# First cross-attention of a decoder: another job order, another bank table, and the maximum in two pairs of heads

## What is computed

```python
y_dca, y_main = y[:, -16:, :], y[:, :-16, :]
q = ln((x @ Wq + bq) by head)            # 16 heads of 32
k, v = ln(y_main @ Wk + bk), y_main @ Wv + bv
k_dca, v_dca = ln(...), ...              # the last 16 rows of the context, weights of their own
ctx     = softmax(q k.T * scale) v          # over 240 keys
ctx_dca = softmax(q k_dca.T * scale) v_dca  # over 16 keys
x = layernorm(x + (ctx + ctx_dca) @ Wo + bo)
```

## Time and profile before

| | us |
|---|---|
| median of 3 runs | 2538.05 |
| the profiled execution | 2538.91 |
| its span, first to last instruction | 2537.0 |
| main loop of the first cross-attention | 505 to 990 of the span |

### The profile page before, as it was taken

One profiled execution on the slowest core, in us unless ns is written; L12 is line 12 of the kernel. 1 busy time (PEld: TensorE's weight loads), 2 busy tenths in 40 slices (PEclk: granted clock), 3 DMA queues, 4 the chain that ended last, 5 costly groups with the idle time before them and its releaser, 6 DMA issues. The chain is left out here.

```text
span 2537.0 us, 40781 instructions
## 1 busy us (share of the span) xinstructions
PE 2159.8 (85%) x15664; PEld 1831.0 (72%) x15664; DVE 1568.4 (62%) x3131; ACT 1215.2 (48%) x3223; POOL 762.9 (30%) x820
## 2 busy tenths in 40 slices
PE   5999998388888887499997879999999999966876
PEld 5898897266777766377776778888988988853443
DVE  3555664555656554788875645556666666656777
ACT  3555553366666653444333334445555554423466
POOL 2233332666666652044441111111111112220011
PEclk8999999689999987599998989999999999988999
DMA  3000000200000000711101031224324312101000
GB/s 133 1 2 1 2 1 1 75 5 5 5 5 6 5 1 4 256 65 34 34 18 46 1 133 59 93 84 145 113 84 146 112 68 76 51 1 67 6 29 34
DMA packets 42777, 127.17 MB, mean 50 GB/s; under 512 B 3917, under 2 KB 11086, under 8 KB 37593
## 3 DMA queue, kind: packets, MB, share of 16 engines
q1 hardware_dynamic: 42584, 124.56, 14.0%
HBM read 103.57 MB, written 20.97 MB: 49 GB/s over the span
## 5 line engine op out<-in xcount | busy, mean ns | idle before, releaser
L2003 POOL TENSOR_TENSOR x_probs<-x_probs,x_total 128x512 f32<-128x512 f32 x128 | 133.2, 1041 | 595.5 <-DVE x_total L1973 595.3
L1928 ACT ACTIVATE x_probs<-banks,x_nmax 128x256 f32<-128x256 f32 x256 | 119.0, 469 | 213.9 <-DVE x_nmax L1962 213.9
L133 ACT ACTIVATE x_probsT_hi<-banks 128x512 fp32r<-128x512 f32 x256 | 143.7, 607 | 106.8 <-PE banks L1862 101.2
L519 PE MATMUL banks<-x_probsT_hi,x_V_hi 128*128 128x256 f32 x512 | 160.6, 314 | 38.6 <-DVE x_probsT_lo L139 38.0
L139 DVE TENSOR_TENSOR x_probsT_lo<-banks,x_probsT_hi 128x512 fp32r<-128x512 f32 x256 | 165.1, 675 | 45.8 <-ACT x_probsT_hi L133 45.6
L519 PE MATMUL banks<-x_turned,x_wq_hi 128*128 128x256 f32 x1024 | 186.0, 283 | 8.2 <-DVE x_turned L139 8.2
L925 ACT ACTIVATE x_probs<-banks,x_nmax 128x240 f32<-128x240 f32 x256 | 114.4, 460 | 139.8 <-DVE x_nmax L955 139.8
L817 POOL TENSOR_TENSOR x_probs<-x_probs,x_total 128x960 f32<-128x960 f32 (+1 forms) x128 | 130.4, 1040 | 161.3 <-DVE x_total L967 161.3
L448 ACT ACTIVATE a_probs<-banks,a_nmax 128x128 f32<-128x128 f32 (+1 forms) x256 | 104.1, 419 | 126.9 <-DVE a_nmax L464 126.9
L519 PEld LDWEIGHTS banks<-x_turned,x_wq_hi 128*128 128x128 f32 x1024 | 156.8, 189 | 9.4 <-DVE x_turned L139 9.4
L504 POOL TENSOR_TENSOR a_probs<-a_probs,a_total 128x512 f32<-128x512 f32 x64 | 93.9, 1467 | 229.5 <-DVE a_total L474 229.5
(11 more groups left out here) (455 smaller groups left out, 7245.6 us busy)
## 6 DMA issues: line engine op xcount, KB each, us to landing
x_turned<-x_parked SPq DMA_DIRECT2D x24, 1536.0 KB, 6.8
x_parked<-x_turned SPq DMA_DIRECT2D x8, 1536.0 KB, 5.8
x_raw_q<-in_L_xattn_Wq_dram SPq DMA_DIRECT2D x5, 1024.0 KB, 5.2
x_raw_o<-in_L_xattn_Wo_dram SPq DMA_DIRECT2D x5, 1024.0 KB, 8.2
x_all<-in_x_dram SPq DMA_DIRECT2D x2, 2048.0 KB, 18.7
x_ys<-in_ctx_dram SPq DMA_DIRECT2D x16, 256.0 KB, 2.9
f_raw<-in_L_ffn_W_g_dram SPq DMA_DIRECT2D x4, 1024.0 KB, 7.0
f_raw<-in_L_ffn_W_u_dram SPq DMA_DIRECT2D x4, 1024.0 KB, 5.4
```

The lines of the kernel that those rows point to most:

```text
L133: return eng.activation(out, in_, ACT.Copy, scale=scale)
L519: ins = eng.matmul(out, lhs, rhs, start=start and n == 0, stop=stop and n == len(steps) - 1)
L1928: ins = eng.activation(probs[t][r][:, j, :], g.S[:, 2 * t + r, j * S:(j + 1) * S], ACT.Exp, bias=nmax[:, t, r, j:j + 1], accum_out=total[: ...
L2003: eng.tensor_tensor(probs[t][r][:, :, :], probs[t][r][:, :, :], total[:, t, r, :].unsqueeze(2).to_broadcast([P, 2, S]), ALU.mult).then_inc ...
```

## The change

Three things, all in cross_attention_0. The list of jobs is written out as one flat list in another order. The bank of each job is written out as a table (`banks`) in place of bank_turns. The maximum of a unit over the 240 keys is taken by two instructions, two heads each, that raise the semaphore max once each; ACT waits for the first ahead of heads 0 and 1 and for the second ahead of heads 2 and 3. The arithmetic is the same.

Some of what moves, in the new list: pt(7,0) and pt(7,1) of the batch before come ahead of qt(1); av(3) of the batch before comes ahead of score(1), right behind q(0); kl(1) goes from behind v(0) to behind av(0); yt is ahead of pt(2,0); pt(1,0) ahead of out(0) and exp(2), pt(1,1) behind; k(0) and kn(0) come ahead of exp(4); k(1) goes from ahead of score(5) to behind it; q(1) is behind pt(5,1); pt(5,0) and pt(5,1) come ahead of exp(6); xt(1) is between pt(6,0) and pt(6,1), xt(0) behind qt(0); kl(0) is behind scale(7); fin(1) is last; load comes ahead of exp(6).

```diff
@@ -531,26 +531,23 @@
     NU = 2 * KD
     NP = 2
 
-    def unit(u):
-        return [(("score", u), 0), (("max", u), 0), (("exp", u), 0)]
-
-    def turned(u, shift=0):
-        return [(("pt", u, kt), shift) for kt in range(QT)]
-
-    def ready(u):
-        return [(("rec", u), 0), (("scale", u), 0)]
-
     order = [
-        [(("ql", 0), 0), (("qt", 1), 0), *turned(7, -1), *unit(0), (("q", 0), 1), (("ql", 1), 0), *ready(0)],
-        [*unit(1), (("qn", 0), 1), (("av", 3), -1), *ready(1), *turned(0), (("kt", 1), 0), (("v", 0), 0), (("kl", 1), 0)],
-        [*unit(2), (("v", 1), 0), *ready(2), *turned(1), (("out", 0), -1)],
-        [*unit(3), (("out", 1), -1), (("fin", 0), -1), (("av", 0), 0), *ready(3), *turned(2), (("yt",), 1), (("load",), 2)],
-        [*unit(4), (("k", 0), 1), (("fin", 1), -1), *ready(4), *turned(3), (("k", 1), 1)],
-        [*unit(5), (("kn", 0), 1), (("av", 1), 0), *ready(5), *turned(4)],
-        [*unit(6), (("kn", 1), 1), (("q", 1), 1), *ready(6), *turned(5)],
-        [(("score", 7), 0), (("kt", 0), 1), (("max", 7), 0), (("exp", 7), 0), (("qn", 1), 1), (("av", 2), 0), (("kl", 0), 1),
-         *ready(7), *turned(6), (("xt", 0), 2), (("xt", 1), 2), (("qt", 0), 1)]]
-    steps = [((s, *job), shift) for s, jobs in enumerate(order) for job, shift in jobs]
+        (("pt", 7, 0), -1), (("pt", 7, 1), -1), (("qt", 1), 0), (("ql", 0), 0), (("score", 0), 0), (("ql", 1), 0),
+        (("max", 0), 0), (("exp", 0), 0), (("rec", 0), 0), (("q", 0), 1), (("av", 3), -1), (("score", 1), 0),
+        (("max", 1), 0), (("scale", 0), 0), (("exp", 1), 0), (("rec", 1), 0), (("pt", 0, 0), 0), (("pt", 0, 1), 0),
+        (("qn", 0), 1), (("kt", 1), 0), (("v", 0), 0), (("score", 2), 0), (("max", 2), 0), (("scale", 1), 0),
+        (("v", 1), 0), (("pt", 1, 0), 0), (("out", 0), -1), (("exp", 2), 0), (("rec", 2), 0), (("pt", 1, 1), 0),
+        (("score", 3), 0), (("max", 3), 0), (("scale", 2), 0), (("out", 1), -1), (("fin", 0), -1), (("exp", 3), 0),
+        (("av", 0), 0), (("kl", 1), 0), (("yt",), 1), (("rec", 3), 0), (("scale", 3), 0), (("pt", 2, 0), 0),
+        (("pt", 2, 1), 0), (("score", 4), 0), (("max", 4), 0), (("k", 0), 1), (("kn", 0), 1), (("exp", 4), 0),
+        (("rec", 4), 0), (("pt", 3, 0), 0), (("pt", 3, 1), 0), (("score", 5), 0), (("max", 5), 0), (("exp", 5), 0),
+        (("rec", 5), 0), (("scale", 4), 0), (("k", 1), 1), (("av", 1), 0), (("pt", 4, 0), 0), (("pt", 4, 1), 0),
+        (("scale", 5), 0), (("score", 6), 0), (("max", 6), 0), (("kn", 1), 1), (("pt", 5, 0), 0), (("pt", 5, 1), 0),
+        (("load",), 2), (("exp", 6), 0), (("rec", 6), 0), (("q", 1), 1), (("score", 7), 0), (("kt", 0), 1),
+        (("max", 7), 0), (("exp", 7), 0), (("av", 2), 0), (("rec", 7), 0), (("scale", 6), 0), (("pt", 6, 0), 0),
+        (("xt", 1), 2), (("qn", 1), 1), (("scale", 7), 0), (("pt", 6, 1), 0), (("qt", 0), 1), (("xt", 0), 2),
+        (("kl", 0), 1), (("fin", 1), -1)]
+    steps = [((0, *job), shift) for job, shift in order]
     slots, tail = grouped_slots(steps)
     front = [("load", 0), ("yt", 0), ("load", 1), ("xt", 0, 0), ("xt", 0, 1), ("k", 0, 0), ("k", 0, 1), ("q", 0, 0), ("q", 0, 1),
              ("kn", 0, 0), ("kn", 0, 1), ("kt", 0, 0), ("qn", 0, 0), ("qn", 0, 1), ("kl", 0, 0), ("xt", 1, 0), ("xt", 1, 1),
@@ -558,14 +555,26 @@
     ring = ("xt", "yt", "q", "k", "v", "qt", "kt", "pt", "av", "out")
     halves = ("xt", "yt", "v", "pt", "av", "qt", "kt")
     lows = ("xt", "yt", "q", "k", "v", "pt", "av", "out")
-    turn = bank_turns([(job[0], *job[2:]) for job in slots[1] if job[0] in ring])
+    banks = [
+        [
+            ("qt", 1), ("v", 0), ("out", 0), ("pt", 2, 1), ("pt", 3, 1), ("pt", 4, 0), ("q", 1), ("pt", 6, 0),
+            ("xt", 0)],
+        [
+            ("pt", 7, 1), ("av", 3), ("pt", 0, 0), ("v", 1), ("out", 1), ("yt",), ("k", 1), ("pt", 5, 1), ("av", 2),
+            ("xt", 1)],
+        [
+            ("pt", 0, 1), ("pt", 1, 0), ("av", 0), ("k", 0), ("pt", 3, 0), ("av", 1), ("pt", 5, 0), ("kt", 0),
+            ("qt", 0)],
+        [
+            ("pt", 7, 0), ("q", 0), ("kt", 1), ("pt", 1, 1), ("pt", 2, 0), ("pt", 4, 1), ("pt", 6, 1)]]
+    turn = {job: n for n, jobs in enumerate(banks) for job in jobs}
     temps = {(job[0], *job[2:]): n for n, job in enumerate(j for j in slots[1] if j[0] in ("q", "k", "qt", "kt"))}
     bank_frees = {kind: ("high" if kind in ("qt", "kt") else "low", kind) for kind in ring}
     temp_frees = {"q": ("low", "q"), "k": ("low", "k"), "qt": ("lowered", "ql"), "kt": ("lowered", "kl")}
     plan = Plan(
         front, slots, tail,
         events={"full": dict.fromkeys(ring, 1), "high": dict.fromkeys(halves, 1), "low": dict.fromkeys(lows, 1),
-                "lowered": {"ql": 1, "kl": 1}, "score": {"score": 1}, "max": {"max": 1}, "shift": {"max": 1}, "exp": {"exp": 1},
+                "lowered": {"ql": 1, "kl": 1}, "score": {"score": 1}, "max": {"max": 2}, "shift": {"max": 1}, "exp": {"exp": 1},
                 "rec": {"rec": 1}, "scale": {"scale": 1}, "loaded": {"load": 16}, "square": {"q": 1, "k": 1},
                 "affine": {"qt": 1, "kt": 1}, "power": {"qn": 1, "kn": 1}, "normal": {"qn": 1, "kn": 1},
                 "stats": dict.fromkeys(("q", "k", "out"), 1), "rooting": {"out": POOL_ROOT_STEPS}, "root": {"out": 1},
@@ -920,8 +929,9 @@
                     eng.activation(normal[kind + str(a[0])][:, :], bank, ACT.Copy).then_inc(squared, 1)
                 if kind == "exp":
                     u, = a
-                    eng.wait_ge(maxed, plan.done("max", b, "max", u))
                     for r in range(G4):
+                        if r % 2 == 0:
+                            eng.wait_ge(maxed, plan.done("max", b, "max", u) - 1 + r // 2)
                         eng.activation(probs[u % NP][:, r, 0:MAIN], g.S[:, r, 0:MAIN], ACT.Exp,
                                        bias=nmax[:, u, r:r + 1], accum_out=total[:, u, 0, r:r + 1])
                     eng.wait_ge(dshifted, plan.done("shift", b, "max", u))
@@ -952,7 +962,8 @@
                     u, = a
                     eng.wait_ge(scored, plan.done("score", b, "score", u))
                     eng.tensor_copy(dscore[:, :, :], g.S[:, :, MAIN:S]).then_inc(linked, 1)
-                    eng.tensor_reduce(nmax[:, u, :], g.S[:, :, 0:MAIN], AX.X, ALU.max, negate=True).then_inc(maxed, 1)
+                    for pair in (slice(0, 2), slice(2, 4)):
+                        eng.tensor_reduce(nmax[:, u, pair], g.S[:, pair, 0:MAIN], AX.X, ALU.max, negate=True).then_inc(maxed, 1)
                     n = plan.start("link", b, 2, "max", u)
                     eng.wait_ge(linked, n + 1)
                     eng.tensor_reduce(dmax[:, u, :], dscore[:, :, :], AX.X, ALU.max, negate=True).then_inc(linked, 1)
```

## The result

The changed kernel takes 2495.24 us (median of 4 runs, 2494.56 to 2496.74) against 2538.66 us in the runs beside it: a ratio of 0.983, 95% interval 0.9813 to 0.9847, 43 us faster. The forecast was 2525 us with a range of 2506 to 2548: the direction was right, the gain was 3.3 times the forecast's 13 us, and the time lies under the range.

The account below looks back on a forecast made before the run. No engine is full; PE is nearest. Per batch, 49 us of PE work plus 8.0 of waits make 57.0, plus 2.5 for the clock 59.5; against 61.1, eight batches gain 13 us: 2525 us, range 2506 to 2548.

Parts of the forecast that it names:

- The wait that the split goes at: ACT waits 139.8 us for the maximum in 61 of 64 units; splitting gains 32 us at most, loses 6 at worst.
- The last rival: ACT comes late to the split maximum, so it isn't used; order alone gives about 2530 us, inside the forecast's chance 0.43.
- The sum of 57.0 us: Main loop's period in the new order without a slow stretch: PE's work plus 8.0 us of waits, against 60.2 before.
- seven named waits: PE's waits per batch: pt(0,0) 0.7, score(4) 0.4, score(5) 2.8, xt(1) 1.8, pt(7,0) 0.7, qt(1) 1.1, score(7) 0.2 us.
- 49 us of work: PE's job times at full clock, added over one batch of the loop; no order can go under it.
- The clock: A 6.8 us slow stretch behind the wait ahead of score(5), running into k(1) and av(1), loses 2.5 us a batch.
- the rival with the clock up: Clock stays up or falls only where PE waits anyway: period 57.0, gain 33 us, 2505 us; chance 0.18.
- The first and last batches: Both have holes in any order and were given the same gain as the middle ones, 1.6 us each.
- The old order at full clock: Period 60.2 us without a slow stretch, taking 1.3 of the 2.4 us that av(2) loses as lost.
- The rule on rotating banks: Independent groups should rotate through banks; k(0) and pt(3,0) shouldn't be neighbours, or the period could be 1.9 us longer.
- The rule on the clock going to and fro: Short idle times between groups cycling through banks make PE's clock go to and fro, and each change is paid.
- The slow rival: Idle pieces at k(0) and av(2) drop the clock twice for 6.8 us: period 63.8, 2560 us; chance 0.17.

Follow-up runs that it names:

- e6_one_wait: The changed kernel with ACT waiting for both pairs of the maximum ahead of head 0: 2506.93 us.
- e7_filled: The changed kernel with seven overwritten matmuls of 512 columns ahead of pt(3,0), where PE waits 1.9 us: 2488.94 us.
- e1_split_only: The kernel before, old order and old banks, with only the maximum split into two pairs: 2525.36 us.
- e11_before_filled: The kernel before with four overwritten matmuls ahead of kt(0), where PE waits 1.0 us: 2531.15 us, against 2535.01 beside it.
- e3: The changed kernel with the banks given out in turn, as before, in place of the table: 2492.56 us.
- e4: The changed kernel with k(0) in bank 1 behind yt instead of bank 2: 2496.86 us.
- e10: The changed kernel with exp(4), rec(4) and scale(4) ahead of k(0), and the banks in turn: 2492.35 us.
- e5_exp4_first: The changed kernel with exp(4), rec(4) and scale(4) ahead of k(0) and kn(0), and k(0) in bank 3: 2494.25 us.

## Why the prediction was wrong

- **The wait that the split goes at, and what it is worth.** Right. I said that ACT's 139.8 us aren't PE's, and priced the split far under its 32 us; alone it brings 12. The half at 650 ns (646), the added wait at nothing and DVE's extra instructions at nothing all held (e6_one_wait).
- **The last rival had the split giving almost nothing,** with the order alone at 2530 against 2525. It was wrong on the split and on the size: 30 us are the order's and 12 the split's.
- **The sum of 57.0 us. This step failed too.** Its list of waits was right: five of the seven named waits are in the trace at their places, four of them ended by what was named; score(4) waits only 0.1, score(7) not at all. But they were up to 0.7 us too long, and the 49 us of work a little too small. In a batch without a slow stretch (616.39 to 672.18, above) PE is busy for 50.0 us and idle for 5.8, where 49 and 8.0 were summed. So the period came out at 57.0 where 55.8 is measured, 1.2 us a batch too long; the two errors in part cancel. A part of it can be that I summed durations where neighbours on an engine overlap (two halves of the maximum, 646 ns each, take 1.21 us together).
- **The clock. This is the step that failed by most.** "A slow stretch of the same 6.8 us there" with "2.5 us lost" in every batch. There was one at that place, but 3.4 us long, costing 1.4, and not in every batch: of the measured 56.85, 1.05 us is the clock's. On eight batches that is 12 us too dear. The cause was right: with the hole filled (e7_filled) the clock stays up.
- **How the 30 us between 2525 and 2495 divide.** Seven periods were each 2.7 us shorter than forecast: 10 us in all by the clock's term, 8.5 by the sum of waits. The last batch gave 6 us more than forecast, the front 0.6, and 4 to 5 lie outside the stage. With the clock's term alone put right (12 us in eight batches) the forecast would have been 2513, inside its range; with the waits too, 2504. All of these erred the same way. That the time is nearest to 2505, the figure of the rival with the clock up, is luck: the clock did fall, and the 57.0 behind that figure is the same overlong sum.
- **"The first and last batches have holes in any order; I give them the same gain."** At 1.6 us the last batch was priced too low. It gave 7.7 us with its tail (66.8 us from its score(0) to the end of the stage, for 74.5). I take it that, with no next batch's work in it to cover a wait, each sooner exp and scale counts; that wasn't tried by itself. The split alone took 3.9 of it (70.6 us in e1_split_only).
- **The old order at full clock.** 60.2 said, 59.8 measured (e11_before_filled): of the 2.4 us that av(2) lost, 1.7 were lost to the batch (61.5 less 59.8) and not 1.3.
- The remaining 4 to 5 us of the 43 lie outside the stage, at least in the profiled execution, in parts with the same code. What there is of it in the medians isn't settled.
- **The rule on rotating banks**, of the Trainium skill, Perfetto Trace Analysis, Optimizing Tensor Performance (Matmuls), stood against the table. The trace has the waits that it warns of (1.9 and 1.4 us a batch), and three experiments (e3, e4 and e10) show that removing them gives at most 2 or 3 us: each lies over another wait that ends at nearly the same time. By the runs, keeping to it neither hurts nor helps here.
- **The rule on the clock going to and fro**, of the Trainium skill, TensorE: Matmul & The Clock Gate, A second HAM failure mode, holds, and the trace has it in both kernels (six and five falls in six periods); its price, 1.4 us for a fall of 3.4 us, is smaller than the 2.5 that I took.
- The slow rival (0.17) had two stretches of 6.8 us on PE's path. Nothing of that came. Adding a worst hole, a worst stretch and a worst place for it, as I did, makes a sum that no row asked for.

## What to carry to other kernels

Where engines take their jobs in order from one list, the waits of the new order can be worked out from the durations of the old one, to about 1 us in 57 here; sum them with the overlap of neighbours on an engine, and price the first and last rounds by themselves: the last one here gave 7.7 us where a middle one gave 4.3. Before removing the wait that is shown ahead of a job, look for the one just under it: the waits of 1.9 and 1.4 us for a bank, when removed, gave nothing clear of the noise, for another releaser came within 0.5 us of the same moment, and an exp made 0.7 us sooner was given back at a bank two units later. A maximum taken in two parts pays if the consumer starts on the first part; two instructions with one wait bring nothing.

## What the runs showed of the hardware

A hole of about 2 us in PE's work costs more than itself: a stretch of 3.4 us at half clock behind it, and 1.4 us of the period. Filling it with 1.8 us of matmuls whose result is thrown away took 6 us off the kernel (2488.94 for 2495.24) and 1.1 us off the period. The stretch doesn't follow each hole of the same length: in the changed kernel the holes of seven batches are alike, and five of them are followed by one. Two holes of 0.85 and 0.67 us with k(0) and the transposes between them (e5_exp4_first) had none behind them in seven batches. In the kernel before a stretch of 6.8 us, in which PE does the work of 3.4 us at full clock, cost only 1.7 us of a period (61.5 against 59.8 in e11_before_filled); I take it that the rest fell on waits for other engines, which isn't shown. What decides between the batches isn't settled here.
